# RWKV-6 mixer with a ternary feed-forward, one core: only the first feed-forward weight is quantised ahead of tile 0

## The reference

```
xx  = shifted(x) - x
mix = tanh((x + xx * time_maa_x) @ maa_w1)          # 5 ranks of 32
mw, mk, mv, mr, mg = einsum(mix, maa_w2)
k = (x + xx*(maa_k+mk)) @ Wk.T     # v, r, g alike; w gives the decay
S = decay * S + k^T v ; y = r (S + u k^T v)         # per head of 32
x = layernorm(x + (groupnorm(y) * ln_g + ln_b) * g @ Wo.T)

gamma = mean(|W|) + 1e-6                            # for W_fc and for W_proj
Wq    = sign(W) * min(round(|W| / gamma), 1)
h = gelu(x @ Wq_fc.T)                               # 2048 wide
h = layernorm(h, ln_w, ln_b)
x = layernorm(x + h @ Wq_proj.T)
```

## Time and profile before

| | us |
|---|---|
| median of 3 runs (lowest, highest) | 3076.63 (3074.3, 3081.04) |
| the profiled execution, its time | 3077.73 |
| the profiled execution, its span | 3075.9 |
| mean granted TensorE clock (share of full) | 0.991 |
| busy: TensorE, VectorE, ScalarE, GpSimd | 2895.1, 2488.6, 1928.0, 931.3 |

### The profile page before, as it was taken

How to read it: one execution, slowest core, us unless ns; L and a number is a source line. 1 busy time by engine, 2 the same in 40 slices (tenths; PEclk the granted TensorE clock), 3 DMA queues, 4 the chain that set the end, 5 groups by cost and what they waited for, 6 DMA issues and landing times.

```text
span 3075.9 us, 101635 instructions
## 1 busy us (share of the span) xinstructions
PE 2895.1 (94%) x40249; PEld 2120.9 (69%) x40249; DVE 2488.6 (81%) x5435; ACT 1928.0 (63%) x4079; POOL 931.3 (30%) x790
## 2 busy tenths in 40 slices
PE   1889999999999999999999999999999999999997
PEld 0666677777677777677777676777677777767775
DVE  8467887788887788888788898788798788888777
ACT  0456676666676666676666576666567666667664
POOL 1223232333322333332233322233323233332232
PEclk9899999999999999999999999999999999999999
DMA  5000000000000000000000000000000000000000
GB/s 215 8 15 23 13 19 23 22 16 22 13 23 19 23 16 23 16 20 19 23 16 22 16 19 19 23 15 22 23 13 19 23 22 16 23 13 23 19 23 15
DMA packets 22822, 73.40 MB, mean 24 GB/s; under 512 B 3104, under 2 KB 3360, under 8 KB 20768
## 3 DMA queue, kind: packets, MB, share of 16 engines
q1 hardware_dynamic: 22432, 67.10, 6.4%
HBM read 50.31 MB, written 16.78 MB: 22 GB/s over the span
## 4 chain that ended last, share of the span: by engine, by line
PE 63%; DVE 23%; issue 9%; ACT 3%; DVEq 1%; DMA 1%; SPq 0%; ACTq 0%; POOLq 0%; POOL 0%
PE psP L404 18%; PE psF L641 11%; PE psP L442 7%; PE psP L616 6%; PE psF L660 4%; DVE HLO L1351 4%; DVE ARENA L1226 2%; PE psY L522 2%; PE psY L538 2%; DVE SUMS L1343 2%; DVE ARENA L1100 2%; DVE ARENA L1088 2%; DVE ARENA L1166 2%; DVE ARENA L1290 1%; PE psP L424 1%
## 5 line engine op out<-in xcount | busy, mean ns | idle before, releaser
L404 PE MATMUL psP<-ARENA,WALL 128*128 128x256 f32 x3072 | 694.2, 381 | 2.7 <-ACT ARENA L733 2.7
L690 ACT ACTIVATE ARENA<-ARENA 32x512 f32<-32x512 f32 (+3 forms) x930 | 524.2, 564 | 188.1 <-DVE ARENA L1166 92.5
L404 PEld LDWEIGHTS psP<-ARENA,WALL 128*128 128x128 f32 x3072 | 574.9, 190 | 79.3 <-issue 1.8
L1351 DVE SCALAR_TENSOR_TENSOR HLO<-GG,FWB,HHI 128x128 f16<-128x128 f32 x1024 | 347.5, 400 | 283.4 <-ACT HHI L861 278.4
L641 PE MATMUL psF<-XHI,WFC 128*128 128x128 f16 x4096 | 488.2, 220 | 2.2 <-DVE ST L1367 1.9
L641 PE MATMUL psF<-XLO,WFC 128*128 128x128 f16 x4096 | 486.6, 220 | 0.0
L902 POOL TENSOR_TENSOR MT<-ARENA 32x256 fp32r<-32x256 f32 x330 | 319.3, 968 | 445.3 <-ACT ARENA L690 416.7
L916 POOL TENSOR_TENSOR ARENA<-ARENA,XT 128x1024 f32<-128x1024 f32 x128 | 278.6, 2177 | 506.3 <-DVE ARENA L1100 506.3
L641 PEld LDWEIGHTS psF<-XHI,WFC 128*128 128x128 f16 x4096 | 397.9, 98 | 41.0 <-issue 32.9
L641 PEld LDWEIGHTS psF<-XLO,WFC 128*128 128x128 f16 x4096 | 402.0, 98 | 17.6 <-issue 10.3
L660 PE MATMUL psF<-WPJ,HHI 128*128 128x512 f16 x1024 | 390.6, 381 | 13.5 <-ACT GG L852 13.5
(11 more groups left out here) (165 smaller groups left out, 5160.4 us busy)
## 6 DMA issues: line engine op xcount, KB each, us to landing
XT<-x_ch SPq DMA_DIRECT2D x33, 520.0 KB, 3.4
ARENA<-x_tok SPq DMA_DIRECT2D x32, 512.0 KB, 4.7
out<-OUT SPq DMA_DIRECT2D x64, 256.0 KB, 2.1
WALL<-w_all SPq DMA_DIRECT2D x5, 1024.0 KB, 15.5
ARENA<-wfc SPq DMA_DIRECT2D x4, 1024.0 KB, 8.2
ARENA<-wpj SPq DMA_DIRECT2D x3, 1024.0 KB, 14.8
GG<-wpj SPq DMA_DIRECT2D x1, 1024.0 KB, 18.9
OUT<-w2a SPq DMA_DIRECT2D x8, 64.0 KB, 14.0
```

Of the source, the lines that this page charges most:

```text
L404: mm = pe.matmul(psP[:, P.bank(f"{name}{g}"), COLS * c:COLS * (c + 1)], WALL[:, w, k, 128 * (2 * g + c):128 * (2 * g + c + 1)], cc(XF[slot ...
L690: return act.activation(o, i, ACT.Copy)
L1351: e = dve.scalar_tensor_tensor(out=HLO[:, k, :], in0=GG[:, u % 2, 0, 128 * m:128 * (m + 1)], scalar=FWB[:, 0, k:k + 1], in1=HHI[:, k, :], ...
```

## The change

Set-up: the small steps on ln_w and ln_b, with VHI and VLO, come first. Only the first weight is summed and quantised ahead of tile 0. The mixing weights are loaded with five broadcast loads in place of 20, right after the first weight and tile 0's input, under a semaphore of their own; the second weight is loaded last. The raw chunks change places: the first weight's lie at the end of ARENA1 and in ARENA2, the second's in ARENA1's first 6144 columns and GG. GpSimd splits the mixing weights as soon as they are there; the state is zeroed behind that.

Tile 0: the second weight's magnitudes are summed behind `mixed_by_x` (two chunks) and behind "mv" (two), its mean is taken on TensorE ahead of "mr", chunks 4 and 5 are quantised behind "mr", 6 and 7 behind "mg", ARENA1 is zeroed after chunk 6, and both engines that write RB wait for that. `against_second` is cut in eight groups of eight matmuls, one behind each level and four between the later steps, into psF; the two copies (WSUM, BSUM) come at the tile's end. The centring of the value weight moves behind `mixed_by_x`.

```diff
@@ -193,8 +193,8 @@
         VMEAN = SUMS[:, 1, 0:KC * HEADS]
-        RAW = ([ARENA1[:, 2048 * k:2048 * (k + 1)] for k in range(4)] + [ARENA2[:, 2048 * k:2048 * (k + 1)] for k in range(3)]
-               + [GG[:, :, :, :].rearrange("p i s n -> p (i s n)")])
+        RAW = ([ARENA1[:, 6144:8192]] + [ARENA2[:, 2048 * k:2048 * (k + 1)] for k in range(3)]
+               + [ARENA1[:, 2048 * k:2048 * (k + 1)] for k in range(3)] + [GG[:, :, :, :].rearrange("p i s n -> p (i s n)")])
@@ -203,7 +203,7 @@
-        const_in, weights_in, values_in = sem("const_in"), sem("weights_in"), sem("values_in")
+        const_in, mixing_in, weights_in, values_in = sem("const_in"), sem("mixing_in"), sem("weights_in"), sem("values_in")
         raw_in = [sem(f"raw_in{k}") for k in range(8)]
@@ -264,7 +264,7 @@
         NPL = len(LEVELS) + 2
-        NWEIGHTS = 8 + 5 * 4
+        NMIXING, NWEIGHTS = 1 + 5, 7
@@ -284,18 +284,19 @@
                 sp.dma_start(RAW[k], wfc[:, 2048 * k:2048 * (k + 1)]).then_inc(raw_in[k], 16)
+            sp.dma_start(XT[:, :, :], x_ch[0]).then_inc(xt_in, 16)
+            sp.dma_start(W1[:, :, :], w1).then_inc(mixing_in, 16)
+            for f in range(5):
+                rank = w2a[rows(f), :] if f < 4 else w2b
+                sp.dma_start(W2RAW[f // 2][:, f % 2, :], rank.unsqueeze(0).broadcast_to([4, MIXR, C])).then_inc(mixing_in, 16)
+            sp.dma_start(WALL[:, W_V, :, :], w_all[:, W_V, :, :]).then_inc(values_in, 16)
+            for dst, src in ((TD1[:, :, :], td1), (TD2[0:DECR, :], td2), (TD2[DECR:2 * DECR, :], td2),
+                             (WALL[:, W_K, :, :], w_all[:, W_K, :, :])):
+                sp.dma_start(dst, src).then_inc(weights_in, 16)
+            for w in (W_R, W_G, W_O):
+                sp.dma_start(WALL[:, w, :, :], w_all[:, w, :, :]).then_inc(weights_in, 16)
             for k in range(4):
                 sp.dma_start(RAW[4 + k], wpj[:, 2048 * k:2048 * (k + 1)]).then_inc(raw_in[4 + k], 16)
-            sp.dma_start(XT[:, :, :], x_ch[0]).then_inc(xt_in, 16)
-            sp.dma_start(WALL[:, W_V, :, :], w_all[:, W_V, :, :]).then_inc(values_in, 16)
-            for dst, src in ((W1[:, :, :], w1), (TD1[:, :, :], td1),
...
@@ -331,30 +332,33 @@
+            pe.wait_ge(const_in, 16 * 4)
             pe.wait_ge(su_dve, 1)
-            pe.wait_ge(const_in, 16 * 4)
-            pe.matmul(psP[:, 0, 0:1], ONES, SC[:, 8:9], start=True, stop=True).then_inc(su_pe, 1)
+            pe.transpose(psX[0:2, 0:128], SC[:, 10:12], IDENT).then_inc(su_pe, 1)
             pe.wait_ge(su_dve, 2)
-            pe.matmul(psP[:, 1, 0:1], ONES, SC[:, 9:10], start=True, stop=True).then_inc(su_pe, 1)
-            pe.wait_ge(su_dve, 3)
-            pe.transpose(psX[0:2, 0:128], SC[:, 10:12], IDENT).then_inc(su_pe, 1)
...
             pe.matmul(psY[:, 0:1], ONES[0:2, :], SC[0:2, 14:15], start=True, stop=True)
             pe.matmul(psY[:, 1:2], ONES[0:2, :], SC[0:2, 15:16], start=True, stop=True).then_inc(su_pe, 1)
-            def against_second(v):
-                for m in range(MH):
-                    for part, h in enumerate((VHI, VLO)):
...
+            pe.wait_ge(su_dve, 4)
+            pe.matmul(psP[:, 0, 0:1], ONES, SC[:, 8:9], start=True, stop=True).then_inc(su_pe, 1)
+            def second_magnitude():
+                pe.wait_ge(su_dve, 6)
+                pe.matmul(psF[:, 0, 0:1], ONES, SC[:, 9:10], start=True, stop=True).then_inc(su_pe, 1)
+            def against_second(v, part):
+                if part == 0:
+                    pe.wait_ge(su_dve, 3)
+                    pe.wait_ge(quantised, 8)
+                for m in range(MH // 4 * part, MH // 4 * (part + 1)):
+                    for n, h in enumerate((VHI, VLO)):
+                        mm = pe.matmul(psF[:, v, :], h[:, v, m:m + 1].broadcast_to([128, 128]), WPJ[:, m, :],
+                                       start=(m == 0 and n == 0), stop=(m == MH - 1 and n == 1))
+                if part == 3:
+                    mm.then_inc(su_pe, 1)
+            pe.wait_ge(mixing_in, 16 * NMIXING)
@@ -372,7 +376,6 @@
             tanh_argument("w1b").then_inc(tm_first, 1)
-            against_second(1)
@@ -389,6 +392,7 @@
             mix(-1, 0, "mw", lambda name: None)
+            pe.wait_ge(weights_in, 16 * NWEIGHTS)
@@ -434,7 +438,11 @@
                     ffn.up(0, 0)
+                if first:
+                    second_magnitude()
                 mix(it - 1, 3, "mr", wait_free)
+                if first:
+                    pe.wait_ge(su_dve, 5)
                 pe.wait_ge(xf_ready, 5 * it + 3)
@@ -485,6 +493,8 @@
                         ffn.down(0, i)
+                    if first:
+                        against_second(0, i)
@@ -551,9 +561,13 @@
                     ffn.up(1, 0)
+                if first:
+                    against_second(1, 0)
                 from_chunk(1)
...
                     ffn.up(1, 1)
+                if first:
+                    against_second(1, 1)
@@ -574,6 +588,8 @@
                     ffn.up(1, 2)
+                if first:
+                    against_second(1, 2)
                 values(1)
@@ -584,6 +600,8 @@
                     ffn.up(1, 3)
+                if first:
+                    against_second(1, 3)
                 pe.wait_ge(deviations, it + 1)
@@ -633,6 +651,8 @@
                         pe.wait_ge(w_dve, W.read(j, f"xt{p}"))
+                        if first:
+                            pe.wait_ge(su_dve, 7)
                     name = f"fc{g}_{p}"
@@ -711,8 +731,7 @@
-            act.wait_ge(su_dve, 6)
-            act.wait_ge(su_pool, 2)
+            act.wait_ge(quantised, 4)
             act.wait_ge(tm_first, 1)
@@ -758,6 +777,8 @@
                 act.wait_ge(p_act, P.read(it, "r1"))
+                if first:
+                    act.wait_ge(su_pool, 2)
                 for p in range(PAIRS):
@@ -873,14 +894,7 @@
         def _(pool):
-            pool.wait_ge(quantised, 4)
-            pool.memset(ARENA1[:, 0:6144], 0.0).then_inc(su_pool, 1)
-            pool.wait_ge(quantised, 8)
...
+            pool.wait_ge(mixing_in, 16 * NMIXING)
             for i in range(3):
@@ -903,6 +917,9 @@
             pool.wait_ge(w2_split, 6)
+            pool.wait_ge(quantised, 4)
+            pool.memset(ARENA2[:, 0:512], 0.0).then_inc(su_pool, 1)
+            pool.wait_ge(su_pool, 1)
             mix_low(-1, 0, 10)
@@ -926,6 +943,9 @@
                             ffn.late_normed()
+                if first:
+                    pool.wait_ge(quantised, 7)
+                    pool.memset(ARENA1[:, 0:6144], 0.0).then_inc(su_pool, 1)
                 if ffn:
@@ -1015,67 +1035,78 @@
             dve.wait_ge(const_in, 16 * 4)
-            for i in range(2):
-                for k in range(4):
+            dve.tensor_reduce(SC[:, 10:12], FWB[:, :, :], AX.X, ALU.max, apply_absolute_value=True).then_inc(su_dve, 1)
+            dve.wait_ge(su_pe, 1)
+            dve.tensor_reduce(SC[0:2, 12:13], psX[0:2, 0:128], AX.X, ALU.max).then_inc(setup_step, 1)
+            dve.wait_ge(setup_step, 1)
+            dve.tensor_scalar(SC[0:2, 14:16], IDENT[0:2, 0:2], SC[0:2, 12:13], None, ALU.mult).then_inc(su_dve, 1)
+            dve.wait_ge(su_pe, 2)
+            dve.tensor_scalar(AMAX, psY[:, 0:2], 1e-30, None, ALU.max).then_inc(setup_step, 1)
+            dve.wait_ge(setup_step, 2)
+            dve.reciprocal(SC[:, 2:4], AMAX).then_inc(setup_step, 1)
+            dve.wait_ge(setup_step, 3)
+            dve.tensor_scalar(FWB[:, 0, :], FWB[:, 0, :], SC[:, 2:3], None, ALU.mult)
+            dve.tensor_scalar(FWB[:, 1, :], FWB[:, 1, :], SC[:, 3:4], None, ALU.mult).then_inc(setup_step, 1)
+            dve.wait_ge(setup_step, 4)
+            dve.tensor_copy(VHI[:, :, :], FWB[:, :, :]).then_inc(setup_step, 1)
+            dve.wait_ge(setup_step, 5)
+            dve.tensor_tensor(VLO[:, :, :], FWB[:, :, :], VHI[:, :, :], ALU.subtract).then_inc(su_dve, 1)
+            dve.tensor_scalar(PAR[:, :, LN_G:LN_B + 1], PAR[:, :, LN_G:LN_B + 1], 0.5, None, ALU.mult)
+            def magnitudes(i, chunks, total):
+                for k in chunks:
                     dve.wait_ge(raw_in[4 * i + k], 16)
...
                 e.then_inc(setup_step, 1)
-                dve.wait_ge(setup_step, i + 1)
-                dve.tensor_reduce(SC[:, 8 + i:9 + i], RED[:, 128 * i:128 * (i + 1)], AX.X, ALU.add).then_inc(su_dve, 1)
-            dve.tensor_reduce(SC[:, 10:12], FWB[:, :, :], AX.X, ALU.max, apply_absolute_value=True).then_inc(su_dve, 1)
...
+                if total:
+                    dve.wait_ge(setup_step, total)
+                    dve.tensor_reduce(SC[:, 8 + i:9 + i], RED[:, 128 * i:128 * (i + 1)], AX.X, ALU.add).then_inc(su_dve, 1)
+            def thresholds(i, mean, n):
+                dve.wait_ge(su_pe, 3 + i)
+                dve.tensor_scalar(SC[:, 16 + i:17 + i], mean, 1.0 / (C * HID), GAMMA_EPS, ALU.mult, ALU.add).then_inc(setup_step, 1)
+                dve.wait_ge(setup_step, n + 1)
```

(45 more changed lines are left out.)

53 lines of the change are left out of this document (removed).

## The result

Before: median 3075.68 us (four runs, 3074.30 to 3081.04). After: median 3054.22 us (four runs, 3052.76 to 3057.01), a ratio of 0.9927 with a 95% interval of 0.9915 to 0.9939: faster by 0.7%, some 21 to 22 us. The forecast was 3052, the range 3036 to 3066.

A forecast was written before the change was run, and what follows sets the result against it. Bound: the set-up until 93.8 us is one VectorE chain, and tile 0 has no feed-forward beside it. Sum: 3077.73 - 37.8 (set-up) + 14.0 (first half) - 1.0 (second half) = 3052.9, as a median 3052; range 3036 to 3066.

The forecast's parts named there:

- Reductions and thresholds: Set-up on VectorE: four reductions end at 17.9, total and thresholds take about 1.5, so quantising starts at 19.4, not 31.56.
- GpSimd's hold-up, 9.0: Set-up: GpSimd's splits of the mixing weights delay VectorE's quantising by all 9.0 us, so the first weight ends at 43.2.
- they are in at about 20: Set-up: at some 420 GB/s, with 6.7 MB ahead of the last, the six loads GpSimd awaits arrive at about 20 us.
- Rival (a): Engines do not hold each other up in quantising: 3043 without the set-up's 9.0, 3033 without tile 0's 10.4 too; chance 0.20.
- the second weight is in at 46, its last two chunks are read at 63: nothing.: Set-up loads: issues on the SP queue only reordered, 15 fewer; the second weight arrives before it is read, costing nothing.
- Tile 0's first half, 14.0: VectorE's second-weight quantising, held by GpSimd's additions and fill, makes the even queries 14.0 us late; bounds 3.6 and 16.
- Second half, -1.0: Tile 0: eight groups of second-weight products fill holes and tile 0's matmuls get shorter: -1.0 us, between -3 and +4.0.
- The rule by which each group would start at the lower clock after the wait: Tile 0's second half: all eight groups cost 3.4 us each instead of 1.7, 13.6 more in all, giving 3066.
- rival (b): More exposed in tile 0: groups precede waiting products, half at lower clock (6.8), or six loads late: 3058 to 3068; chance 0.12.
- (c): Slower: TensorE stays at its lower clock through tile 0, from the key products on: 3099 us; chance 0.03.
- (d): No change: tile 0's stall and groups eat all but 6 of the 37.8 gained: 3081, or half that, 3067; chance 0.05.
- Last copies, nothing: Tile 0's end: the last two copies (1.4) fall in VectorE's wait for GpSimd's root: nothing, or 1.4 without that cover.

The follow-up runs named there:

- loads in pieces: Changed kernel with the five broadcast loads of the mixing weights made twenty of 64 KB, in the same place: 3047.26 us.
- small fill: Changed kernel with GpSimd's fill in tile 0 cut from 6144 to 64 columns, leaving out most of the zeros: 3045.67 us.
- no sums: Changed kernel with 60 of the 64 products against the second weight left out: 3064.36 us.
- waits for the sums: Changed kernel with 60 of the 64 second-weight products replaced by 120 TensorE waits on a semaphore already reached: 3053.74 us.
- same count: Changed kernel with all 64 second-weight products reading the first slice, so as many instructions but other sums: 3053.42 us.
- late splits: Changed kernel with 20 load pieces, all second-weight reductions behind "mv", zeros on ScalarE, and GpSimd's splits waiting for the mixing input: 3043.15 us.

## Why the prediction was right

The sign, the path and the total held: 3054.2 against 3052, the row root 24.5 earlier against 24.8 (37.8 - 14.0 + 1.0). Two of its terms did not, and they cancelled, so the closeness of the total is in part luck. By its steps:

**Reductions and thresholds.** Quantising starts at 18.78, forecast 19.4. Right.

**GpSimd's hold-up, 9.0: mis-sized, and in the changed kernel nought in quantising.** Quantising ended at 33.6, not 43.2, because the splits had not begun. The step that failed is "they are in at about 20": the rate of 420 GB/s was taken for every load, whatever its shape. What was left of the hold-up fell on the mixing input, 2.45 us instead of the 1.67 forecast. With loads that do land early the hold-up was 5.5: VectorE stood longer in five instructions, but GpSimd's own were held in turn (4.26 for a subtraction that took 2.40 in the kernel before), so not all of its time fell on VectorE. The Trainium skill, "SBUF — State Buffer", section "Who interferes with whom", has whichever starts first keep the shared ports for its whole instruction while the other waits; the alternation of 3.00 and 3.25 with 4.26 agrees with that. The fill's rows cannot show the order: both starts lie 0.02 us apart (93.99 and 94.01), and VectorE was the one held. Rival (a), no hold-up, was right about the changed set-up's rows and wrong about the reason.

**"the second weight is in at 46, its last two chunks are read at 63: nothing."** It cost VectorE the 8.93 us before 51.94. This error, 9 too little, cancels the one above, 9 too much, both from the same slow loads; so the set-up's gain came out at 37.1 against 37.8. The total was right partly by this accident. With the loads in pieces both are put right together, and the first mixed group comes 4.6 us earlier.

**Tile 0's first half, 14.0.** Measured 12.4 at the queries and 14.1 at the first level (112.71 against 135.77, 23.06 earlier), as forecast where the levels begin. The fill's share was exact: 6.32 for the conversion, and 5.0 back when it was taken away, by the small fill and by the zeros on ScalarE alike. "mg" stood directly behind a select (86.93). The two selects that met GpSimd's additions took 3.02 and 4.14, a conversion 2.98. What the forecast did not have is the part between queries and levels, 10.1 us instead of 8.4: the first products after TensorE's wait of 7.31 took 3.64 us at a granted clock of 0.50, where they took 2.14 at 1.00 before.

**Second half, -1.0: right in size, only in part by the reason given.** Measured -1.46. The forecast had the groups fill holes and make tile 0's own matmuls shorter. The first part holds: the levels took 1.10 each with the groups between them, at a granted clock of 1.00, and the doubled products, which find no hole left, cost their full length. The second part is not shown. Without the groups the second half was 40.5 us, already 4.7 shorter than the 45.2 before: the clock was higher than before (0.87 for 0.74) without them, and the products for the next input took 1.99 us instead of 3.78. Then the groups added 3.2. Why the clock was higher there than in the kernel before stays open; with waits in the groups' place it was 0.80 and the half took 43.7.

The rule by which each group would start at the lower clock after the wait holds for the keys' products (the 3.64 above) and part of the gate group behind them, which had paid for the wait when the groups came: their products are 0.216 apart from the start. Where the groups were missing, the third and the fourth level came behind 1.88 and 0.85 us without work and took 1.94 and 1.93 at a granted clock of 0.50. That is the behaviour which the Trainium skill, "TensorE: Matmul & The Clock Gate", section "HAM oscillation — how this bites in real kernels", describes, and the trace without the sums agrees. Of rival (b) one condition came true, the six loads landed some 15 us late, but not its time, since the delay took the hold-up away; its lower clock in the groups did not occur. (c) and (d) fall with the 0.216 and the total.

**Last copies, nothing.** From the next tile's decay products to the row root nothing moved (24.52 earlier at both). Tile 1 is 1.7 longer than before, and the other tiles and the end give 1.5 back. In all fourteen profiles tile 1 took 93.7 or more where its first 16 products of k took 5.3 to 5.4 us (eight kernels, clock 0.53 or 0.54), and 92.1 where they took 3.69 (six kernels, clock 1.00). So tile 1's difference is TensorE's clock; why it falls in some executions stays open, the wait ahead of the products being 1.37 us in all.

**Still open.** What in the code sets the loop's period. The work in it does not (no sums against waits for the sums), nor does the data (same count), nor one wait on GpSimd. The longer tiles lose their time at one place, in the products for the variance and next to them, where TensorE waits for nothing that the profile shows. That fits a delay in the supply of its instructions, but this is argued: a kernel that only moves the loop's instructions in memory was not tried. The period of 91.8 with the late splits has another place: there ScalarE waited for those products only 0.7 us in 27 tiles. Where it comes from was not told apart.

## What to carry to other kernels

Cost a load by its shape, not only by its bytes: one load with four broadcast copies outermost was slower than four plain ones, and everything queued behind it was late. Work moved between two engines that hold each other up is priced by what runs beside it at its new place: 5.03 us for one fill, nothing for the same zeros on a third engine. And when a kernel is a loop of thirty tiles, read the loop's period before reading an edit in its prologue: 0.4 us of period cost 12.3 us, as much as the best set of edits tried here gained at the loop's entry. Read the clock there too: a root that moves by 2 us between two single profiles is not yet the effect of an edit.

## What the runs showed of the hardware that was not expected

- Five broadcast loads ran at 90 to 101 GB/s, the same bytes in twenty loads at 246 to 266.
- The tile period went from 91.6 us to 92.0 when 60 matmuls that run once, ahead of the loop, were taken out, to 92.3 when 64 were added, and back to 91.6 when waits took their place.
- Those longer tiles lose their time at one place: ScalarE waited 16.6 us for the products for the variance (60 matmuls fewer) and 30.2 us (64 more), against 3.0 us in the changed kernel.
- 64 more products in tile 0's second half cost 13.57 us, where the first 60 cost 3.2 against a kernel without them and nothing against one with waits in their place. With them all four levels took 1.10 us; without them the third and the fourth took 1.94.
- The same 32 products, behind the same code, took 7.14, 8.64 and 10.13 us in three kernels' profiles; 16 later ones took 3.69 us at a granted clock of 1.00 or up to 5.38 at 0.53.
